# Eight experts' feed-forward part on one core: all experts for all tokens, against tokens scattered to their two experts in 46 tiles of 128 slots

## The chip, the core and the metric

One core of one Trainium2 chip. The time is that of one whole execution on the device in microseconds (us); several executions are timed and their median is given. Engines: TensorE (PE; its weight loads are PEld), VectorE (DVE), ScalarE (ACT), GpSimd (POOL), and SyncE (SP), which issues DMAs. A small q behind an engine's name means its sequencer.

## What is computed

x has 4 x 512 tokens of 256 features, all fp32. The first half is attention with 16 heads (4 key/value heads) of 128: softmax attention with rotary positions and a gated linear recurrence, averaged, projected back, added to x and normalised. The second half, which the change rewrites, is:

```python
routing_weights = softmax(x @ gate_w.T)              # 8 experts
top_w, top_idx = top_k(routing_weights, 2)
comb[t, top_idx] = top_w                             # zero for the six others
g = einsum('td,edf->etf', x, w_gate)                 # F = 176 features an expert
u = einsum('td,edf->etf', x, w_up)
y = einsum('etf,efd->etd', silu(g) * u, w_down)
out = layernorm(x + einsum('te,etd->td', comb, y))
```

## The kernel before

The five engines have a program each, written in order, and meet only at semaphores. Most fp32 products are done as three fp32r products: of the high parts, and of each high part with the other's low part (`_hi`, `_lo`). So each operand needs a copy that rounds to the high part and a subtraction that makes the low part.

**Attention.** 16 groups g (4 batches by 4 key/value heads), 4 steps c of 128 tokens each; unit u = 4g + c. Group 0 and group 15 are written out, groups 1 to 14 are a loop on each engine. In a step TensorE does, in this order: `score` (L405, L414), `gla_matrix` (L423), `gate_sums` (L375), `project` of step c+2 (L362), `output` of step c-1 (L434), `turn_weights` (transposes of the softmax weights, L443), `turn` (transposes of q, k for the next step, L386 to L395), `gather` (L452, L461) and the state's update (L465). VectorE: row maxima (L838), scaling of the weights (`normalise`, L872), `add_output` into `acc` (L903), and the low parts; its step ends with `k_out`, `q_low` and `log_gates`. GpSimd: `weigh_features` (L1227), `move_v`, `decay` (L1239), `rotate` (L1216, L1219), `x_split`. In groups 0 and 15 `decay` (L893) and `move_v` are VectorE's instead. In group 15 GpSimd splits the FFN's weights (L1273, L1280), loaded by SP, and VectorE and GpSimd normalise the first 512 tokens.

**FFN.** Four groups n of 512 tokens; the 8 x 176 features are taken as 11 blocks f of 128, which cut across experts. For each (n, f) TensorE computes `gate_up` (12 matmuls of 512 columns, L547), spreads the routing weights over the features (`spread_comb`, L555) and adds `down` of block f-2 (12 matmuls of 256 columns, L567) in PSUM bank PR. ScalarE: silu (L757) and the high part of h (L763). VectorE: two products (L1090, L1096) and the low part (L1102). Each group's normalisation and routing (transposes, logits, rank of each expert L1067 to L1072, weights) run between the blocks of the group before. The last group's sum, second normalisation and two output DMAs follow the last `down` (L1183 to L1202, L337 to L340).

## Time and profile before

| | us |
|---|---|
| runs | 1077.69, 1073.81, 1077.68; median 1077.68 |
| profiled execution | 1077.24 |
| its span, first to last instruction | 1075.5 |
| busy: PE, PEld, DVE, ACT, POOL | 1007.1, 802.7, 759.4, 627.2, 633.1 |
| mean granted TensorE clock | 0.988 |

The span is the profile's; the time of an execution is 1.7 us more. Matmuls overlap, so what a matmul costs is read from the distance of two starts and not from its duration. An idle time in square brackets stands ahead of the instruction, with what ended it. The three attention groups before group 15 go from 655.5 to 807.5 us, counted by `add_output`; the FFN's first matmul starts at 858.87.

### The profile page before, as it was taken

How to read it: one execution, taken by the hardware profiler on the slowest of the kernel's cores; microseconds unless marked ns; L12 is line 12 of the kernel's file. 1: busy time of each engine (PE TensorE's matmuls, PEld its weight loads, DVE VectorE, ACT ScalarE, POOL GpSimd, SP SyncE). 2: the span in 40 equal slices, each digit the busy share in tenths (PEclk: the TensorE clock that was granted, in tenths of full speed). 3: DMA queues.
4: the chain of work that ended last, by engine and by line, in shares of the span. 5: the costliest groups of instructions: out<-in, count | busy, mean ns of one | idle time of the engine just before them, and what ended most of it. 6: DMA issues, size and time to landing. Idle time of an engine off the chain costs nothing.

```text
span 1075.5 us, 20731 instructions
## 1 busy us (share of the span) xinstructions
PE 1007.1 (94%) x5860; PEld 802.7 (75%) x5860; DVE 759.4 (71%) x1741; ACT 627.2 (58%) x1944; POOL 633.1 (59%) x656
## 2 busy tenths in 40 slices
PE   4699999999999999999999999999997999999996
PEld 3567777677777777777777776777775688888886
DVE  4888767677676767676767776776769765767655
ACT  4456666666766667666666666667665334333321
POOL 5678676767666767676676767676659560202000
PEclk8899999999999999999999999999999999999999
DMA  7110000000000000000000000000002110000001
GB/s 234 50 50 25 11 10 10 10 10 15 10 10 10 10 10 10 10 11 13 10 10 10 10 10 10 10 15 10 25 0 74 58 45 1 1 21 1 20 1 40
DMA packets 26095, 24.07 MB, mean 22 GB/s; under 512 B 1744, under 2 KB 22608, under 8 KB 25936
## 3 DMA queue, kind: packets, MB, share of 16 engines
q1 hardware_dynamic: 26064, 23.67, 7.3%
q8 instruction: 17, 0.28, 0.1%
q14 instruction: 14, 0.11, 0.0%
HBM read 21.57 MB, written 2.10 MB: 22 GB/s over the span
## 4 chain that ended last, share of the span: by engine, by line
PE 79%; DVE 12%; ACT 5%; issue 3%; DMA 0%; DVEq 0%; POOLq 0%; POOL 0%; SPq 0%
PE OA L461 11%; PE S L547 11%; PE PR L362 10%; PE S L414 8%; PE S L443 6%; PE MS L434 6%; PE PR L567 6%; PE OA L452 4%; PE OA L423 4%; DVE pr L872 3%; ACT eqk L671 3%; PE PR L390 3%; PE PR L386 2%; PE MS L375 2%; DVE qd L893 2%
## 5 line engine op out<-in xcount | busy, mean ns | idle before, releaser
L644 ACT ACTIVATE pr<-S,nm 128x128 f32<-128x128 f32 (+3 forms) x256 | 131.5, 524 | 94.4 <-DVE nm L838 92.6
L1239 POOL TENSOR_TENSOR qd<-eqk,eg 128x512 f32<-128x512 f32 x56 | 68.0, 1215 | 177.9 <-issue 151.7
L461 PE MATMUL OA<-wT,V 128*128 128x512 f32 x320 | 149.3, 596 | 1.4 <-DVE wT L920 1.4
L671 ACT ACTIVATE eqk<-qkv,nmx 128x128 f32<-128x128 f32 x320 | 124.3, 395 | 8.4 <-DVE nmx L912 8.3
L1216 POOL TENSOR_TENSOR rp<-qkv,cos 128x640 f32<-128x640 f32 x64 | 100.8, 1575 | 30.9 <-ACT qkv L661 22.4
L838 DVE TENSOR_REDUCE nm<-S 128x2 f32<-128x256 f32 (+3 forms) x128 | 101.9, 818 | 21.8 <-PE S L414 20.0
L872 DVE TENSOR_SCALAR pr<-pr,rl 128x128 f32<-128x128 f32 (+3 forms) x256 | 110.2, 473 | 4.5
L461 PEld LDWEIGHTS OA<-wT,V 128*128 128x128 f32 x320 | 59.5, 190 | 72.1 <-issue 68.9
L1219 POOL TENSOR_TENSOR rp<-rp,rt 128x640 f32<-128x640 f32 x64 | 99.0, 1547 | 5.0
L1216 POOL TENSOR_TENSOR rt<-qkv,sin 128x640 f32<-128x640 f32 x64 | 98.9, 1545 | 0.0
L443 PE MATMUL S<-cm,pr 128*128 128x128 f32 x640 | 81.9, 275 | 15.7 <-DVE pr L872 15.7
L692 ACT COPY wT<-S 128x512 f32<-128x512 f32 x96 | 51.7, 592 | 67.5 <-PE S L443 67.5
L443 PEld LDWEIGHTS S<-cm,pr 128*128 128x128 f32 x640 | 71.4, 142 | 19.1 <-DVE pr L872 19.1
L362 PE MATMUL PR<-w_hi,ring_hi 128*128 (+2 forms) x256 | 78.0, 386 | 7.8 <-DVE w_lo L1131 6.9
L1227 POOL TENSOR_TENSOR eqk<-eqk,rse 128x640 f32<-128x640 f32 x56 | 72.2, 1290 | 20.8 <-PE OA L461 10.6
L763 ACT CAST wo_hi<-eqk 128x512 fp32r<-128x512 f32 x44 | 27.3, 620 | 90.2 <-DVE eqk L1096 90.2
L1310 POOL TENSOR_TENSOR rstd<-ve,neghalf 128x4 f32<-128x4 f32 x7 | 7.2, 1024 | 123.1 <-DVE ve L1031 123.1
L434 PE MATMUL MS<-wo_hi,oT_hi 128*128 (+1 forms) x256 | 74.1, 289 | 5.4 <-DVE gc L880 5.4
L362 PE MATMUL PR<-w_hi,ring_lo 128*128 (+2 forms) x256 | 73.7, 370 | 0.0
L434 PE MATMUL MS<-wo_hi,oT_lo 128*128 (+1 forms) x256 | 72.3, 282 | 0.0
L434 PE MATMUL MS<-wo_lo,oT_hi 128*128 (+1 forms) x256 | 72.2, 282 | 0.0
L547 PE MATMUL S<-ring_hi,w_hi 128*128 128x512 f32 x176 | 70.3, 399 | 0.0
(180 smaller groups left out, 2972.9 us busy)
## 6 DMA issues: line engine op xcount, KB each, us to landing
xraw<-in_x_cols SPq DMA_DIRECT2D x64, 128.0 KB, 2.2
stage<-in_wffn SPq DMA_DIRECT2D x11, 384.0 KB, 3.1
stage<-in_wqkv SPq DMA_DIRECT2D x6, 384.0 KB, 3.3
acc<-in_x_rows SPq DMA_DIRECT2D x1, 2048.0 KB, 12.6
out<-pr SPq DMA_DIRECT2D x3, 512.0 KB, 2.9
wT<-in_wo_in SPq DMA_DIRECT2D x1, 1024.0 KB, 6.5
pr<-in_wqkv SPq DMA_DIRECT2D x2, 384.0 KB, 4.0
stage<-in_wo_in SPq DMA_DIRECT2D x2, 384.0 KB, 3.2
```

The source lines that it names most:

```text
L362: last = pe.matmul(PR[:, a:b], x[:, cc, k, :], wq_cols(w, kv, k, a, b), start=(i == 0), stop=(i == len(steps) - 1))
L414: last = pe.matmul(S[:, h, 0:n], q[:, h * 128:(h + 1) * 128], k[:, 0:n], start=False, stop=(i == len(steps) - 1), skip_group_check=True)
L434: last = pe.matmul(MS[:, 0:HID], o[:, h * 128:(h + 1) * 128], r, start=(i == 0), stop=(i == len(steps) - 1))
L443: last = pe.transpose(S[:, j, h * 128:(h + 1) * 128], pr[:, h, j * 128:(j + 1) * 128], ident)
L461: last = pe.matmul(OA[:, :], V[:, j, :], wT[:, j, :], start=(c == 0 and j == 0), stop=(j == c))
L547: last = pe.matmul(S[:, 2 * q + q0 % 2, :], w[:, f, k, q, :], x[:, n % 2, k, :], start=(i == 0), stop=(i == len(steps) - 1))
L644: nc.scalar.activation(pr[:, h, 0:n], S[:, h, 0:n], ACT.Exp, bias=nm[:, h:h + 1], scale=1.0, accum_out=ls[:, h:h + 1]).then_inc(s_exp, 1)
L671: last = nc.scalar.activation(eqk[:, par, h * 128:(h + 1) * 128], qkv[:, c % C, h * 128:(h + 1) * 128], ACT.Exp, bias=nmx[:, h:h + 1], sca ...
L838: nc.vector.tensor_reduce(nm[:, 2 * pair:2 * pair + 2], S[:, 2 * pair:2 * pair + 2, 0:n], AX_X, ALU.max, negate=True).then_inc(s_nm, 1)
L872: nc.vector.tensor_scalar(pr[:, h, 0:n], pr[:, h, 0:n], rl[:, h:h + 1], None, ALU.mult).then_inc(s_pn, 1)
L1216: nc.gpsimd.tensor_tensor(to.rearrange("p (h w d) -> p h w d", w=2, d=64), src, tab, ALU.mult).then_inc(s_rt, 1)
L1219: nc.gpsimd.tensor_tensor(rp[:, c % 2, :], rp[:, c % 2, :], rt[:, :], ALU.add).then_inc(s_rp, 1)
```

## The change

- **Routing first.** The loop now covers groups 1 to 11 (`PEEL` = 12); groups 12 to 15 are written out, with step number k = 0 to 15. The first normalisation, transposes, logits, ranks and sums of token tiles 0 to 11 (three batches) are put into these steps at numbered places (`STATS_AT`, `TURN_AT`, ...). Tokens are counted for each expert by a scan and two matmuls (`prefix`), and each expert's slots are rounded up to tiles of 128.
- **Slots.** Set 0 (12 token tiles) has 31 slot tiles, set 1 (4 token tiles) 15: the most that rounding can need. GpSimd scatters each normalised token tile by two indirect DMAs (`send`) to its slots in device memory (`slot_x`), which SP has cleared. 24 of them stand in steps k = 12, 13, 14.
- **FFN by slot tile.** SP loads tile q, TensorE turns it (`turn_x`), reads the tile's expert number from `te` into a register (`value_load`) and uses it to address the weights: `gate_up` 6 matmuls of 352 columns, `turn_h` 2 transposes, `down` 6 matmuls of 256 columns into OA. No work is done on other experts' features. The result goes through ScalarE (`y_out`) and SP to `slot_y`.
- **Gather.** GpSimd fetches the two rows of each token (`fetch`, two indirect DMAs a tile); VectorE adds them with their weights (`combine`), from slot tile 36 on for token tiles 0 to 11; the last four follow all slot tiles. ScalarE does the second normalisation in place.
- **Weights.** The 16 matrices of the experts are split by ScalarE (`wide_high`) and VectorE (`wide_low`) in steps 4 to 14 and after the first tile, no longer by GpSimd. In group 15 GpSimd does `decay` and `move_v` itself.

```diff
+TPB = N // P128
+PEEL = NG - 4
+SETS = ((0, 3 * TPB), (3 * TPB, TILES))
+SLOT_TILES = [((b - a) * P128 * 2 + E * (P128 - 1)) // P128 for a, b in SETS]
+NT_A, NT_B = SLOT_TILES
+NT = NT_A + NT_B
...
+        wide = [("g", 0), ("g", 1), ("d", 0), ("d", 1), ("g", 2), ("g", 3), ("d", 2), ("d", 3),
+                ("g", 4), ("g", 5), ("d", 4), ("d", 5), ("g", 6), ("g", 7), ("d", 6), ("d", 7)]
+        WIDE_AT = (4, 5, 6, 7, 8, 9, 10, 10, 11, 12, 13, 13, 14, 14, 16, 16)
+        n_gu = max(i for i, (kind, _) in enumerate(wide) if kind == "g") + 1
+        TURN_AT = {2: 0, 3: 1, 4: 2, 5: 3, 6: 4, 7: 5}
+        LOGITS_AT = {k + 1: p for k, p in TURN_AT.items()}
+        STATS_AT = {0: 0, 2: 1, 4: 2}
+        NORM_AT = {k + 1: n for k, n in STATS_AT.items()}
+        RANK_AT = {5: 0, 7: 1, 9: 2}
+        EXP_AT = {k + 1: n for k, n in RANK_AT.items()}
+        PREFIX_AT, SLOTS_AT, WEIGH_AT = 10, 11, 13
+        SEND_AT = {12: (0, 4), 13: (4, 8), 14: (8, 12)}
...
+            def clear_slots(s, a, b):
+                sp.dma_start(slot_x[s].rearrange("(n p) d -> p n d", p=P128)[:, a:b, :],
+                             zero[:, :].rearrange("p (o n) -> p o n", o=1).to_broadcast([P128, b - a, HID])).then_inc(s_zf, 16)
...
+            def load_slots(q):
+                if q == 0:
+                    sp.wait_ge(s_sent[0], 16 * 2 * MOST[0])
+                    sp.wait_ge(s_v, NU - 2)
+                    sp.wait_ge(s_rp, NU - 2)
+                    sp.wait_ge(s_gl, NU - 2)
+                if q == NT_A:
+                    sp.wait_ge(s_sent[1], 16 * 2 * MOST[1])
+                later(sp, s_tx, q - 3)
+                sp.dma_start(xg[:, q % 4, :], slot_rows(slot_x, q)).then_inc(s_xg[q % 4], 16)
+            def store_slots(q):
+                sp.wait_ge(s_yo, q + 1)
+                sp.dma_start(slot_rows(slot_y, q), yo[:, q % 3, :]).then_inc(s_y[q % 3], 16)
...
+            def logits(xT, tiles, to):
+                for i in range(tiles):
+                    for k in range(KT2):
+                        last = pe.matmul(to[:, i * E:(i + 1) * E], xT[:, (KT2 * i + k) * 128:(KT2 * i + k + 1) * 128],
+                                         gate_w[:, k * E:(k + 1) * E], start=(k == 0), stop=(k == KT2 - 1))
+                last.then_inc(s_lgm, 1)
...
+                if k in LOGITS_AT:
+                    pe.wait_ge(s_gate, 16)
+                    pe.wait_ge(s_xe, LOGITS_AT[k] + 1)
+                    logits(x1T, 2, MS[:, 256:384])
+                if k == PREFIX_AT:
+                    prefix(0, MS[:, 256:384])
...
+                if k in TURN_AT:
+                    pe.wait_ge(s_am, C * g + c + 1)
+                    turn_tokens(TURN_AT[k], OA)
...
+            def turn_x(q):
+                pe.wait_ge(s_xg[q % 4], 16 * (q // 4 + 1))
+                if q < 2:
+                    pe.wait_ge(s_qdT, NU)
+                    pe.wait_ge(s_rql, 3 * NG)
+                later(pe, s_txl, q - 1)
+                for k in range(KT2):
+                    last = pe.transpose(xside(q)[:, k * 128:(k + 1) * 128], xg[:, q % 4, k * 128:(k + 1) * 128], ident)
+                last.then_inc(s_tx, 1)
+            def gate_up(q):
+                if q == 0:
+                    pe.wait_ge(s_flo, n_gu)
+                    pe.wait_ge(s_te, 1)
+                if q == NT_A:
+                    pe.wait_ge(s_te, 2)
+                expert[q] = pe.value_load(te[0:1, q:q + 1], min_val=0, max_val=E - 1)
+                pe.wait_ge(s_txh, q + 1)
+                pe.wait_ge(s_txl, q + 1)
+                later(pe, s_h, q - 1)
+                steps = [(k, x, w) for k in range(KT2) for x, w in ((xT_hi, gu_hi), (xT_hi, gu_lo), (xT_lo, gu_hi))]
+                for i, (k, x, w) in enumerate(steps):
+                    last = pe.matmul(S[:, q % 2, 0:2 * F], x[:, q % 2, k * 128:(k + 1) * 128],
+                                     expert_cols(w, expert[q], k * 2 * F, (k + 1) * 2 * F),
+                                     start=(i == 0), stop=(i == len(steps) - 1))
+                last.then_inc(s_gu, 1)
+            def turn_h(q):
+                pe.wait_ge(s_h, q + 1)
+                later(pe, s_hl, q - 1)
+                pe.transpose(S[:, 2 + q % 2, 0:128], hbuf[:, q % 2, 0:128], ident)
+                pe.transpose(S[0:TAIL, 2 + q % 2, 128:256], hbuf[:, q % 2, 128:F], ident).then_inc(s_th, 1)
+            def down(q):
+                if q == 0:
+                    pe.wait_ge(s_flo, len(wide))
+                    pe.wait_ge(s_oTl, NU)
+                pe.wait_ge(s_hh, q + 1)
+                pe.wait_ge(s_hl, q + 1)
+                later(pe, s_yo, q)
+                steps = [(k, h, w) for k in range(2) for h, w in ((hT_hi, dn_hi), (hT_hi, dn_lo), (hT_lo, dn_hi))]
+                for i, (k, h, w) in enumerate(steps):
+                    rows = TAIL if k else P128
+                    last = pe.matmul(OA[:, 0:HID], h[0:rows, q % 2, k * 128:(k + 1) * 128],
+                                     expert_cols(w[0:rows], expert[q], k * HID, (k + 1) * HID),
+                                     start=(i == 0), stop=(i == len(steps) - 1))
+                last.then_inc(s_dn, 1)
...
+            for q in range(1, NT + 2):
+                if q + 1 < NT:
+                    turn_x(q + 1)
+                if q < NT:
+                    gate_up(q)
+                if q >= 2:
+                    down(q - 2)
+                if q - 1 < NT:
+                    turn_h(q - 1)
...
+            def x_hi(q):
+                act.wait_ge(s_tx, q + 1)
+                later(act, s_gu, q - 1)
+                nc.scalar.copy(xT_hi[:, q % 2, :], PR[:, (q % 2) * 512:(q % 2) * 512 + 256]).then_inc(s_txh, 1)
+            def silu(q):
+                act.wait_ge(s_gu, q + 1)
+                later(act, s_h, q - 1)
+                nc.scalar.activation(sg[:, q % 2, :], S[:, q % 2, 0:F], ACT.Silu).then_inc(s_sg, 1)
+            def h_hi(q):
+                act.wait_ge(s_th, q + 1)
+                later(act, s_dn, q - 1)
+                nc.scalar.copy(hT_hi[:, q % 2, :], S[:, 2 + q % 2, 0:256]).then_inc(s_hh, 1)
+            def y_out(q):
+                act.wait_ge(s_dn, q + 1)
+                later(act, s_y[q % 3], 16 * (q // 3))
+                nc.scalar.copy(yo[:, q % 3, :], OA[:, 0:HID]).then_inc(s_yo, 1)
...
+            def wide_low(i):
+                dve.wait_ge(s_fhi, i + 1)
+                _, hi, lo, _ = wide_job(i)
+                nc.vector.tensor_tensor(lo, wide_stage(i), hi.bitcast(F32), ALU.subtract).then_inc(s_flo, 1)
...
+                if k in STATS_AT:
+                    moments(STATS_AT[k])
+                if k in RANK_AT:
+                    route_rank(RANK_AT[k], 2 * RANK_AT[k] + 2)
+                    if RANK_AT[k] == 2:
+                        count_before(0)
+                if k == PREFIX_AT:
+                    slot_bases(0)
+                if k == SLOTS_AT:
+                    slots(0)
+                if k == WEIGH_AT:
+                    route_weigh(0)
+                for i in range(len(wide)):
+                    if WIDE_AT[i] == k:
+                        wide_low(i)
...
+            def x_lo(q):
+                dve.wait_ge(s_txh, q + 1)
+                nc.vector.tensor_tensor(xT_lo[:, q % 2, :], PR[:, (q % 2) * 512:(q % 2) * 512 + 256],
+                                        xT_hi[:, q % 2, :].bitcast(F32), ALU.subtract).then_inc(s_txl, 1)
+            def multiply(q):
+                dve.wait_ge(s_sg, q + 1)
+                later(dve, s_th, q - 1)
+                nc.vector.tensor_tensor(hbuf[:, q % 2, :], sg[:, q % 2, :], S[:, q % 2, F:2 * F], ALU.mult).then_inc(s_h, 1)
+            def h_lo(q):
+                dve.wait_ge(s_hh, q + 1)
+                nc.vector.tensor_tensor(hT_lo[:, q % 2, :], S[:, 2 + q % 2, 0:256],
+                                        hT_hi[:, q % 2, :].bitcast(F32), ALU.subtract).then_inc(s_hl, 1)
+            def combine(t):
+                a = acc[:, t, :]
+                dve.wait_ge(s_yg[t % 4], 32 * (t // 4 + 1))
+                nc.vector.scalar_tensor_tensor(out=a, in0=yg[:, t % 4, 0, :], scalar=wts[:, 0, t:t + 1], in1=a, op0=ALU.mult,
+                                               op1=ALU.add).then_inc(s_c0, 1)
+                dve.wait_ge(s_c0, t + 1)
+                nc.vector.scalar_tensor_tensor(out=a, in0=yg[:, t % 4, 1, :], scalar=wts[:, 1, t:t + 1], in1=a, op0=ALU.mult,
+                                               op1=ALU.add).then_inc(s_cb, 1)
+                dve.wait_ge(s_cb, t + 1)
+                norm_stats(2, t)
...
+                if not first:
                     pool.wait_ge(s_cp, C * g + c + 1)
                     pool.wait_ge(s_o, C * g + c)
-                    weigh_features(g, c + 1)
+                    if not (last and c == 3):
+                        weigh_features(g, c + 1)
                     move_v(g, c)
-                    decay(g, c + 1)
+                    if not (last and c == 3):
+                        decay(g, c + 1)
...
+                if k in NORM_AT:
+                    norm1(NORM_AT[k])
+                if k in SEND_AT:
+                    for t in range(*SEND_AT[k]):
+                        send(t)
...
+            def send(t):
+                s = 0 if t < SETS[0][1] else 1
+                if t == SETS[s][0]:
+                    pool.wait_ge(s_sl, s + 1)
+                    pool.wait_ge(s_zf, 64)
+                    pool.wait_ge(s_x1a, SETS[s][1])
+                for r in range(2):
+                    nc.gpsimd.indirect_dma_start(slot_x[s], bass.IndirectOffsetOnAxis(ap=sloti[:, r, t:t + 1], axis=0),
+                                                 acc[:, t, :], None).then_inc(s_sent[s], 16)
+            def fetch(t):
+                if t == 0 or t == SETS[1][0]:
+                    for i in range(3):
+                        pool.wait_ge(s_y[i], stored(NT_A if t == 0 else NT, i))
+                later(pool, s_cb, t - 3)
+                for r in range(2):
+                    nc.gpsimd.indirect_dma_start(yg[:, t % 4, r, :], None, slot_y[0 if t < SETS[0][1] else 1],
+                                                 bass.IndirectOffsetOnAxis(ap=sloti[:, r, t:t + 1], axis=0)).then_inc(s_yg[t % 4], 16)
```

On TensorE, in the middle of the FFN, one block f of before was this; the rows are instructions in order, and L555 is the spreading of the weights.

```order
L555 MATMUL MS<-w_hi,w_lo 128x512
L547 MATMUL S<-ring_hi,w_hi 128x512
L547 MATMUL S<-ring_hi,w_lo 128x512
L547 MATMUL S<-ring_lo,w_hi 128x512
...
L567 MATMUL PR<-wo_hi 128x256
L567 MATMUL PR<-wo_lo,wo_hi 128x256
L567 MATMUL PR<-wo_hi,wo_lo 128x256
```

The three L547 rows stand four times and the three L567 rows four times. A slot tile of after, on the same engine (L686 `down`, L673 `turn_h`, L650 `turn_x`, L665 `gate_up`; ISA and REGISTER_ALU are the sequencer's):

```order
L686 ISA
L686 MATMUL OA<-wo_hi,rq_hi 128x256
L686 REGISTER_ALU
L686 MATMUL OA<-wo_lo,rq_hi 128x256
...
L673 MATMUL S<-cm,rp 128x128
L674 MATMUL S<-cm,rp 48x128
L650 MATMUL PR<-cm,qkv 128x128 x2
L659 TENSOR_LOAD te
L659 ISA x2
L665 ISA
L665 MATMUL S<-w_hi,ring_hi 128x352
```

Twelve matmuls and four transposes stand where 25 matmuls stood, and between `turn_x` and `gate_up` the expert number is loaded. On VectorE the end of a peeled step, k = 9 of after, between its last old instruction (`log_gates`, L1088) and the next step:

```order
L1088 SCALAR_TENSOR_TENSOR gl<-qkv,lnp 128x128
L1131 TENSOR_REDUCE small<-lg 128x4
L1133 TENSOR_TENSOR lx<-lg,small 128x32
L1140 TENSOR_TENSOR rk<-lg 128x256
L1142 TENSOR_TENSOR rk<-lg 128x256
L1143 TENSOR_TENSOR rk<-rk,tri 128x256
L1145 TENSOR_TENSOR rk<-rk 128x256
L1147 TENSOR_REDUCE rank<-rk 128x32
L1150 TENSOR_SCALAR picked<-rank 128x4x8
L1155 SCALAR_TENSOR_TENSOR run<-cm,picked 128x96
L1156 TENSOR_TENSOR before<-run,picked 128x96
L1218 TENSOR_TENSOR w_lo<-stage,w_hi 128x704
```

In before nothing stands there. On GpSimd, steps k = 12 to 14:

```order
L1416 TENSOR_TENSOR rp<-rp,rt 128x640
L1512 DMA slot_x<-acc,sloti 3968x256 x8
L1424 TENSOR_TENSOR eqk<-eqk,rse 128x640
L1445 COPY V<-qkv 128x128
L1436 TENSOR_TENSOR qd<-eqk,eg 128x512
L1440 TENSOR_TENSOR qd<-eqk,eg 128x128
L1413 TENSOR_TENSOR rp<-qkv,cos 128x640
```

Eight indirect DMAs stand ahead of the next step's `weigh_features` (L1424) and `decay` (L1436).

## Rows read from the trace of the kernel before

**Rows 1.** The page's chain that ended last, by engine.

```profile
PE 79%; DVE 12%; ACT 5%; issue 3%; DMA 0%; DVEq 0%; POOLq 0%; POOL 0%; SPq 0%
```

**Rows 2.** Busy us (instructions) of PE, PEld, DVE, ACT, POOL; clock; DMA share, GB/s.

```profile
822.00:860.00 38.00, 31.68 (x158) 23.33 (x159) 32.05 (x75) 16.26 (x46) 26.86 (x30) 0.96 0.21 61
...
910.00:962.00 52.00, 52.00 (x301) 45.62 (x300) 34.65 (x77) 18.42 (x30) 7.36 (x6) 1.00 0.03 11
```

**Rows 3.** Groups by shape from 800 us on: count, busy us, mean ns, idle before.

```profile
L1102 DVE TENSOR_TENSOR wo_lo<-eqk,wo_hi 128x512 fp32r<-128x512 f32 x44 | 31.9, 724 | 30.2 <-ACT wo_hi L763 30.2
...
L763 ACT CAST wo_hi<-eqk 128x512 fp32r<-128x512 f32 x44 | 27.3, 620 | 90.2 <-DVE eqk L1096 90.2
...
L1022 DVE BATCH_NORM_STATS2 st<-acc 128x6 f32<-128x256 f32 x16 | 5.6, 409 | 0.0
...
L1067 DVE TENSOR_TENSOR rk<-lg 128x256 f32<-128x256 f32 x4 | 1.7, 419 | 0.0
```

**Rows 4.** TensorE in order of time: start us, us, line, operation, count.

```profile
452.13 0.60 PE L443 MATMUL S<-cm,pr 128*128 128x128 f32 x4
452.56 0.60 PE L386 MATMUL PR<-cm,rp 128*128 128x128 f32 x4
...
858.87 0.79 PE L547 MATMUL S<-ring_hi,w_hi 128*128 128x512 f32 x1
...
951.78 0.39 PE L547 MATMUL S<-ring_hi,w_hi 128*128 128x512 f32 x1
952.00 0.39 PE L547 MATMUL S<-ring_hi,w_lo 128*128 128x512 f32 x1
...
953.66 0.28 PE L567 MATMUL PR<-wo_lo,wo_hi 128*128 128x256 f32 x1
953.78 0.28 PE L567 MATMUL PR<-wo_hi,wo_lo 128*128 128x256 f32 x1
...
1067.30 0.28 PE L567 MATMUL PR<-wo_hi,wo_lo 128*128 128x256 f32 x1
```

**Rows 5.** VectorE in order of time, `add_output` of units 31, 34, 47, 59, 62.

```profile
452.53 0.42 DVE L903 SCALAR_TENSOR_TENSOR acc<-MS,acc 128x256 f32 x1 [1.86 <-PE MS L434]
...
490.09 0.42 DVE L903 SCALAR_TENSOR_TENSOR acc<-MS,acc 128x256 f32 x1 [0.95 <-PE MS L434]
...
655.50 0.43 DVE L903 SCALAR_TENSOR_TENSOR acc<-MS,acc 128x256 f32 x1 [1.87 <-PE MS L434]
...
807.50 0.42 DVE L903 SCALAR_TENSOR_TENSOR acc<-MS,acc 128x256 f32<-128x256 f32 x1 [0.37 <-PE MS L434]
...
852.39 0.41 DVE L903 SCALAR_TENSOR_TENSOR acc<-MS,acc 128x256 f32<-128x256 f32 x1
```

**Rows 6.** In order of time: last scalings of a step, and TensorE's turning after them.

```profile
437.50 0.88 DVE L872 TENSOR_SCALAR pr<-pr,rl 128x512 f32<-128x512 f32 x2
...
439.00 1.15 PE L443 MATMUL S<-cm,pr 128*128 128x128 f32 x9
...
463.58 1.09 PE L443 MATMUL S<-cm,pr 128*128 128x128 f32 x8 [0.80 <-DVE pr L872]
```

**Rows 7.** Line L362, sequencer's own steps: ns min/median/max, first and last start us.

```profile
L362 PEldq FUSED_REGOPS  x112: 46/51/108, 92.1 to 776.1; - x112
L362 PEldq ALU_OP  x112: 32/32/32, 92.4 to 776.3; - x112
```

**Rows 8.** A GpSimd group of the page; a DMA's landing us; its issue on SP.

```profile
L1216 POOL TENSOR_TENSOR rp<-qkv,cos 128x640 f32<-128x640 f32 x64 | 100.8, 1575 | 30.9 <-ACT qkv L661 22.4
...
xraw<-in_x_cols SPq DMA_DIRECT2D x64, 128.0 KB, 2.2
...
834.14 0.33 SPq L306 DMA_DIRECT2D stage<-in_csel  x1
```

**Rows 9.** VectorE and GpSimd beside each other, in order of time.

```profile
461.01 0.62 DVE L872 TENSOR_SCALAR pr<-pr,rl 128x256 f32<-128x256 f32 x2
...
461.74 1.79 DVE L872 TENSOR_SCALAR pr<-pr,rl 128x256 f32<-128x256 f32 x2
...
461.67 1.29 POOL L1239 TENSOR_TENSOR qd<-eqk,eg 128x512 f32<-128x512 f32 x1 [1.60 <-issue]
```

889 lines of the change are left out of this document (444 added, 445 removed).

## The prediction

> **What bounds the kernel now.** I read first the chain of waits [rows 1]: TensorE holds 79% of the span, VectorE 12%. Then the busy time by stage [rows 2]: in the middle of the feed-forward part (FFN) TensorE is busy 52.00 of 52.00 us, so there only its own work counts. Then the shapes of FFN and routing instructions [rows 3], TensorE in order of time [rows 4], and VectorE's `add_output` (L903), the clock of the attention steps [rows 5]. Three dividing points follow: attention groups 0 to 11 are over at 655.5 us, the last step begins its output near 852.4, the FFN's first matmul starts at 858.9, its last at 1067.3 (over at 1067.6), and the span ends at 1075.5. So the FFN lasts 208.7 us and the tail 7.9. The profiled execution took 1077.24 us, 1.7 above its span; the median of the runs is 1077.68, so a sum made against this execution needs no correction.
>
> In attention three groups last 152.0 us, 50.7 each (655.5 to 807.5) [rows 5]. TensorE has nearly no idle time there, but VectorE is close behind: its last softmax scaling of a step (L872) ends at 438.38 and TensorE's turning of those weights starts at 439.00, 0.6 us of slack, and at step c=1 TensorE already waits 0.80 us for it [rows 6].
>
> **FFN, TensorE's own work.** Starts of matmuls are 0.22 us apart at 512 columns and 0.12 at 256; four transposes take 0.43, so 0.11 each [rows 4]. By the line through the first two, 352 columns cost 0.16. Before, a step f has 12 matmuls of 512, 12 of 256 and the spreading of the weights: about 4.4 us, 44 times. After, a tile of 128 slots has 6 of 352 (0.98), 6 of 256 (0.72) and 4 transposes (0.44): 2.14 us, 46 times, 98 us. If TensorE alone counted, the FFN would fall from 208.7 to about 98.
>
> **FFN, what takes its place.** A tile runs through ScalarE four times and VectorE three, and the output bank OA is single. The loop from one `down` to the next: 6 matmuls 0.72, their drain (a 256-column matmul lasts 0.28 where the next starts after 0.12 [rows 4]) and the hand-over 0.28, `y_out` 0.3 to the start of `h_hi`, `h_hi` 0.4 (a 512-column cast is 0.62 [rows 3], so 0.4 for 256 is an estimate), hand-over 0.06, `h_lo` 0.42 (as L903 [rows 5]), hand-over 0.1 (the hand-overs are estimates): 2.28 us. A second loop is TensorE's sequencer, which stands still at a wait of several semaphores and then issues `down`, `turn_h`, `turn_x`, the load of the expert number into a register, and `gate_up`: 16 matmuls at about 0.055 and some 11 register steps of 0.03 to 0.1 [rows 7], 1.7 us, plus the register load from on-chip memory, L. No such load stands in the trace. Lower bound: a register step, 0.1 us. Upper bound: a 128 KB DMA from issue to landing, 2.2 us [rows 8]. I take L = 1.0, between a local step and a round trip. Period: the longer of 2.28 and 1.7 + L, so 2.7 us; 2.28 at the lower bound, 3.9 at the upper. 46 x 2.7 = 124 us.
>
> The Trainium skill ("DMA: Bandwidth & Descriptors", section "Latency and other measured facts") gives a `tensor_load` a floor of about 600 ns. With that figure the period would be about 2.3 and my sum 18 us lower (an estimate); no row here shows such a load.
>
> On top of 124 come: waiting for the last two expert matrices' low parts before the first `down`, 3; in the first 13 tiles the routing of the last 4 token tiles, about 11 us on VectorE, 4 on TensorE and two table loads on ScalarE, of which I take 10 as exposed; in the last 12 tiles the weighted sum of two gathered rows (two 0.42 and one 0.41 statistics, links between, about 1.4 to 1.9 us on VectorE), which brings the loop over VectorE to about 3.1 us, 5 us more in all. FFN: 142 us, against 208.7: **-67**.
>
> **The four peeled groups.** Groups 0 to 11 keep their code and their 655.5 us; the new constants at the start I cost at nothing (under 1 us if DMA cover is missing). Steps k = 0 to 15 take new work. TensorE: six times 4 transposes (0.43) and 4 small fp32 matmuls (two weight loads of 0.11 each at least, so 0.9, an estimate), prefix sums 1: 9 us. VectorE: three sets of moments (4 x 0.41 and aggregates, 2.1 each), three rankings (five of 0.42 and three of 0.2, 3.0 each), 14 low parts of weights (0.72 for 512 columns, about 0.9 for 704), slot bases 2.1, slots 2.0, weights 1.9: about 36 us [rows 3]. VectorE has room in a step, but these stand at the step's end, ahead of the next step's maxima, where the slack is 0.6 us or less, and some 3.3 only ahead of c=0. Step by step (own work less slack, less what TensorE's new work covers) I get about 22 us exposed for k = 0 to 11 and 6 for 12 to 14. Bounds: 11 if all but TensorE's own work hides, 45 if nothing does. I take **+28**, nearest to the step-by-step row.
>
> GpSimd loses the splitting of weights and in the last group takes the decay products back from VectorE. There from 807.5 to 852.4 go 44.9 us; the same three steps in the steady state (452.53 to 490.09) take 37.6 [rows 5]. **-8** with the little that follows.
>
> **Sending the tokens.** GpSimd issues 24 indirect stores, 8 after each of steps 12, 13, 14, and each batch stands ahead of the next step's `weigh_features` and `decay`, for which TensorE's `turn` waits. GpSimd's chain from step 12's start to `turn_x(0)`: three steps' own work (its rotations are 1.58 us each [rows 8]) and waits 20, landing and first slot load 4.5, so 24.4 + 24T, T being one indirect DMA on GpSimd. TensorE needs about 49 for the same stretch: 6 up to `add_output`, the 37.6 above, 6 exposed. T has no row either: a plain DMA's issue on SP took 0.33 us, and the landing 2.2 [rows 8]. I take T = 1.2, near the middle: 53 against 49, **+5**; nothing at T = 1.0 or less, +28 at 2.2. The clearing of slots (6 MB) and their loads by SP run beside steps of 12 us and four tiles ahead of use: nothing; without that cover a few us.
>
> **The tail.** Last `down`, copy 0.5, store landed 2.4, eight gathers 8T = 9.6, landing 2.2, last sum 1.3, moments, root, shift, normalising 2.3, output 2.7: 21 us against 7.9, **+13**.
>
> **Sum:** 1077.2 - 67 + 28 - 8 + 5 + 13 = 1048, and I say **1049 us**, 2.6% faster.
>
> **Rivals.**
> 1. The register load decides (ends slower). If L is 1.8 us or more the period is 3.5 to 3.9 and the FFN 37 to 55 us longer: 1086 to 1104. It turns slower from a period of 3.3 (L = 1.6). For it: 2.2 us for a DMA; against it: the sequencer's other steps cost 0.03 to 0.1 [rows 7].
> 2. Indirect DMAs are dear on GpSimd: T = 2.2 gives +23 at the sends, +8 in the tail, and gathers slower (4.4 us a tile) than the last tiles, +10: about 1090. For it: when the two engines meet, both are held up: two equal scalings, 0.62 us for the pair, took 1.79 when GpSimd ran beside [rows 9]. The Trainium skill ("SBUF — State Buffer", section "Who interferes with whom") says that GpSimd cannot write descriptors while VectorE runs copies or scalings in a 2-port mode; by that rule VectorE's scalings would lengthen T. The trace agrees that such pairs wait for each other; for descriptors no run shows it yet.
> 3. Everything hides: L under 0.6 and a third of the 28 gone: 1049 - 18 - 9 = 1022.
> 4. The granted clock falls in the FFN to the lower level, as it did for part of the last group (a mean of 0.96 from 822 to 860 us, where TensorE was busy 31.68 of 38 us, against 1.00 in the FFN [rows 2]). At 1.2 GHz a tile is 4.3 us on TensorE: +74, 1123. Against: gaps here are under 1 us each.
>
> **How the numbers follow.** My forecast (1030 to 1072) 0.52, rival 1 0.16, rival 2 0.14, rival 3 0.10, rival 4 0.04, and 0.04 for a mixture near no change. A difference under 0.5% is about what a measurement of this kernel can't tell from none. Faster: forecast and rival 3, 0.61; same 0.07; slower 0.32. The range reaches down to rival 3 and up into rivals 1 and 2: 1020 to 1098; the forecast's own is 1030 to 1072.
>
> **What would show it.** Tiles' first `gate_up` matmuls 2.7 us apart (2.3: L is small; 3.5: rival 1, with TensorE idle by "issue"). The FFN's start near 884 us against 858.9. `add_output` in steps 48 to 59 spread over about 174 us instead of 152. GpSimd's 24 sends ending before TensorE asks for tile 0, or a wait of `turn_x(0)` for it. From the last `down` to the end 21 us. The prediction is wrong if the peeled steps cost over 45 us, or if the period is not set by the sequencer or the loop over OA.

## The result and the profile after

The changed kernel takes 1081.67 us (median of 17 runs, 1078.98 to 1085.5) against 1077.69 for the kernel before: the ratio is 1.0043 with a 95% interval from 1.0025 to 1.0061, so it is 0.4% slower. I had forecast 1049. The profiled execution has a span of 1081.3 us.

The busy time by stage of the kernel after, to be laid beside [rows 2]: groups 1 to 11, peeled steps 0 to 11, the rest of attention, the first 15 slot tiles, the steady tiles, the last ones, the tail. Columns: the stretch and its length; busy us (instructions) of PE, PEld, DVE, ACT, POOL; granted clock; DMA share, GB/s.

```profile
99.10:657.40 558.30, 540.89 (x3212) 421.56 (x3211) 396.77 (x946) 378.62 (x1254) 388.69 (x397) 1.00 0.05 15
657.40:851.20 193.80, 168.64 (x956) 132.17 (x955) 134.46 (x344) 112.27 (x360) 125.65 (x124) 0.94 0.14 43
851.20:908.00 56.80, 46.22 (x215) 35.41 (x214) 33.37 (x79) 26.77 (x77) 38.58 (x39) 0.82 0.29 97
908.00:966.10 58.10, 50.91 (x270) 43.66 (x268) 26.65 (x91) 25.27 (x65) 10.84 (x10) 0.82 0.21 64
966.10:1026.00 59.90, 59.85 (x370) 50.04 (x369) 27.15 (x74) 30.57 (x92) 9.89 (x11) 1.00 0.41 124
1026.00:1051.00 25.00, 21.49 (x126) 16.91 (x124) 20.41 (x65) 12.67 (x38) 19.71 (x21) 1.00 0.55 157
1051.00:1081.30 30.30, 4.50 (x14) 3.08 (x14) 11.03 (x36) 6.61 (x15) 10.91 (x13) 0.51 0.39 124
```

What to see: the feed-forward part (FFN) and tail are 173.3 us instead of 216.6, so it did shrink. But steps 0 to 11 take 193.8 us instead of 152, at a clock of 0.94, and in the two stretches behind them TensorE has both idle time and a clock of 0.82, where [rows 2] showed 0.96 and 1.00. Of the 41.8 us that the steps grew, 20 are TensorE's idle time (25.2 us against 4.9 in the same twelve steps of before) and 21.5 are busy time. My sum had about 9 of these as its new work; the other 12 are what a clock of 0.94 costs over 193.8 us (an estimate: 6% of it).

The chain that ended last, for [rows 1], by engine:

```profile
PE 66%; DVE 15%; ACT 8%; issue 6%; POOL 3%; DMA 1%; DVEq 0%; ACTq 0%; SPq 0%; POOLq 0%
```

TensorE's waits from 657 to 908 us (engine, tile and line, who was waited for: us in total, times, longest):

```profile
PE OA L524 <- DVE oT_lo L960: 16.2, 6, 3.8
PE MS L476 <- DVE gl L1088: 11.3, 4, 3.4
PE PR L650 <- DMA qkv<-slot_x: 2.6, 1, 2.6
...
PE S L544 <- DVE pr L1002: 0.7, 1, 0.7
```

I had looked for the loss at the softmax scaling (`pr`), with 0.6 us of slack [rows 6]. It is not there. TensorE waits for `oT_lo` (which frees bank OA for the next step) and for `gl` (the gates). Both stand close behind the new work: `oT_lo` is the first thing that VectorE does in the steps c=2 and c=3 (in c=0 it comes behind one row maximum), and in a step c=1 the gates come behind two row maxima. Here is VectorE in order of time at the longest of these waits, the turn from step k=5 to k=6 (start us, us, engine, line, operation; in brackets idle time before and its releaser):

```profile
737.40 0.19 DVE L1085 RECIPROCAL rse<-se 128x5 f32<-128x5 f32 x1 [1.09 <-ACT eqk L780]
738.28 0.29 DVE L1088 SCALAR_TENSOR_TENSOR gl<-qkv,lnp 128x128 f32<-128x128 f32 x1 [0.70 <-ACT lnp L793]
...
739.86 1.43 DVE L1143 TENSOR_TENSOR rk<-rk,tri 128x256 f32<-128x256 f32 x1
...
742.47 0.89 DVE L1218 TENSOR_TENSOR w_lo<-stage,w_hi 128x704 fp32r<-128x704 f32 x1
743.27 0.68 DVE L960 TENSOR_TENSOR oT_lo<-OA,oT_hi 128x512 fp32r<-128x512 f32 x1
...
744.01 0.94 PE L524 MATMUL OA<-qdT,kdT 128*128 128x512 f32 x1 [3.84 <-DVE oT_lo L960]
```

VectorE first stands idle for 1.09 and 0.70 us ahead of `rse` and `gl`, then ranks and splits weights from 738.5 to 743.3, and only then makes `oT_lo`, for which TensorE has been waiting 3.84 us. The slack is in the step, and the new work stands behind it. Two smaller things add to it. The ranking product L1143 lasts 1.43 us where its neighbours take 0.42, beside a GpSimd product from 739.75 to 741.01; such holds come up again below. And in two of the twelve steps VectorE waits for ScalarE's high part of a weight matrix, 4.3 us in all, 3.2 of them shortly ahead of a wait of 3.4 us for `gl` at 795: a hand-over that my sum did not have.

### The profile page after: what moved, and what is told of

Same layout as the page of the kernel before. It is cut to its first block, busy times and chain, and to the rows that moved or that the text cites. A ratio compares the mean times of both kernels' runs of the same rounds, so it can differ in the third digit from the quotient of the medians.

```text
span 1081.3 us, 20494 instructions
## 1 busy us (share of the span) xinstructions
PE 962.3 (89%) x5516; PEld 756.3 (70%) x5516; DVE 725.0 (67%) x1772; ACT 643.9 (60%) x2060; POOL 670.9 (62%) x689
## 4 chain that ended last, share of the span: by engine, by line
PE 66%; DVE 15%; ACT 8%; issue 6%; POOL 3%; DMA 1%; DVEq 0%; ACTq 0%; SPq 0%; POOLq 0%
PE OA L562 9%; PE PR L463 9%; PE MS L535 7%; PE S L515 7%; PE S L544 6%; PE OA L686 5%; ACT eqk L780 5%; PE S L665 4%; PE OA L524 3%; PE OA L555 3%; DVE pr L1002 3%; PE PR L491 2%; PE PR L487 2%; PE MS L476 2%; DVE gl L1088 2%
## 5 line engine op out<-in xcount | busy, mean ns | idle before, releaser
L1436 POOL TENSOR_TENSOR qd<-eqk,eg 128x512 f32<-128x512 f32 x59 | 71.9, 1219 | 187.8 <-issue 167.1
L1002 DVE TENSOR_SCALAR pr<-pr,rl 128x128 f32<-128x128 f32 (+3 forms) x256 | 107.4, 462 | 4.5
L1424 POOL TENSOR_TENSOR eqk<-eqk,rse 128x640 f32<-128x640 f32 x59 | 75.8, 1285 | 35.6 <-DVE rse L1085 20.8
L544 PE MATMUL S<-cm,pr 128*128 128x128 f32 x640 | 84.7, 282 | 11.4 <-DVE pr L1002 11.4
L544 PEld LDWEIGHTS S<-cm,pr 128*128 128x128 f32 x640 | 74.4, 145 | 14.1 <-DVE pr L1002 14.0
L524 PE MATMUL OA<-qdT,kdT 128*128 128x512 f32 x128 | 68.6, 618 | 16.3 <-DVE oT_lo L960 16.2
L535 PE MATMUL MS<-wo_hi,oT_hi 128*128 (+1 forms) x256 | 77.1, 301 | 5.0 <-DVE gc L1010 4.5
L535 PE MATMUL MS<-wo_hi,oT_lo 128*128 (+1 forms) x256 | 73.9, 289 | 0.0
L535 PE MATMUL MS<-wo_lo,oT_hi 128*128 (+1 forms) x256 | 73.8, 288 | 0.0
L463 PE MATMUL PR<-w_lo,ring_hi 128*128 (+2 forms) x256 | 70.1, 356 | 0.0
L515 PE MATMUL S<-KT_hi,rq_hi 128*128 128x256 f32 (+2 forms) x192 | 68.9, 359 | 0.0
```

The lines of the kernel that those rows point to most:

```text
L463: last = pe.matmul(PR[:, a:b], x[:, cc, k, :], wq_cols(w, kv, k, a, b), start=(i == 0), stop=(i == len(steps) - 1))
L515: last = pe.matmul(S[:, h, 0:n], q[:, h * 128:(h + 1) * 128], k[:, 0:n], start=False, stop=(i == len(steps) - 1), skip_group_check=True)
L524: pe.matmul(OA[:, :], kdT[:, :], qdT[:, c % 2, :], start=True, stop=True).then_inc(s_at, 1)
L535: last = pe.matmul(MS[:, 0:HID], o[:, h * 128:(h + 1) * 128], r, start=(i == 0), stop=(i == len(steps) - 1))
L544: last = pe.transpose(S[:, j, h * 128:(h + 1) * 128], pr[:, h, j * 128:(j + 1) * 128], ident)
L1002: nc.vector.tensor_scalar(pr[:, h, 0:n], pr[:, h, 0:n], rl[:, h:h + 1], None, ALU.mult).then_inc(s_pn, 1)
```

## Experiments on the peeled steps

**Place within the step.** One version moves the extras, in the same steps: on VectorE `extras(k)` (moments, ranking, slot arithmetic, low parts) from the end of `step` to just ahead of `log_gates` (for c = 0 ahead of `add_output`), on ScalarE `router_exp` and `wide_high` ahead of `weights_out` (the excerpt shows VectorE's part).

```diff
+                if c == 0:
+                    extras(k)
                 ...
                 add_output(...)
                 ...
+                if c:
+                    extras(k)
                 if n2 and c:
                     log_gates(g, c + 2)
-                if k in STATS_AT:
-                    moments(STATS_AT[k])
-                ...
```

> The same work in the same steps, at another place within the step. VectorE's extras stand ahead of the gates' logarithm step, where VectorE waits about 1.6 us a step for ScalarE, instead of behind it (in steps with c = 0 ahead of add_output, where it waits for TensorE); ScalarE's weight copies and router exponentials stand ahead of its copies of the turned weights, where it waits for TensorE, instead of at the step's end. Theory A (place within the step decides): TensorE's waits for oT_lo and gl in steps 48 to 62 fall from about 27 us to under 12, the clock falls less, the feed-forward part starts 15 to 30 us earlier, 1052 to 1067 us. Theory B (VectorE has simply too much to do in these steps, and the place changes only who waits): within 5 us of 1081.7.

Measured: 1063.88 us, ratio to the kernel before 0.9867 [0.9831, 0.9904]; the FFN starts at 890.3 us instead of 908.0. Its waits of TensorE from 659 to 890:

```profile
PE PR L491 <- POOL qd L1446: 9.0, 3, 6.1
PE MS L495 <- DVE acc L1033: 4.4, 4, 2.8
PE OA L524 <- DVE oT_lo L960: 4.2, 2, 2.5
...
PE MS L476 <- DVE gl L1088: 2.1, 3, 0.9
```

The waits for `oT_lo` and `gl` fall from 27.5 to 6.3 us: theory A. No work was taken away, and 18 us are gone. The version moves both engines' extras, so what each engine's move is worth alone is not shown. A new wait came instead, for GpSimd's decay products: 6.11 us at 851.6 where a batch of eight sends stood ahead of them. So the sends, which had cost 2.6 us (one wait of `turn_x`) while other things were late, became the next bound as soon as VectorE was not.

**Less work in the step.** The copies and differences of expert weights cut to 8 columns, everything else as in the changed kernel:

```diff
-                nc.scalar.copy(wide_job(i)[1], wide_stage(i)).then_inc(s_fhi, 1)
+                nc.scalar.copy(wide_job(i)[1][:, 0:8], wide_stage(i)[:, 0:8]).then_inc(s_fhi, 1)
```

> ScalarE's high copy and VectorE's low difference of each of the 16 expert matrices take 8 columns instead of 704 or 512; semaphores, DMAs and everything else stay. Left out: the splitting of the expert weights, so what the feed-forward part multiplies by is not the weights. Theory A (the extras at the end of a step hold up the next step, whoever they are): ScalarE loses 0.76 us and VectorE 0.88 us in each of ten steps, so TensorE's waits of 2 to 4 us for the output low part and for the gates shrink by about 1.5 us each where a matrix stood; the feed-forward part starts 10 to 20 us earlier than 908, the kernel takes 1062 to 1072 us against 1081.7. Theory B (the ranking and the slot arithmetic alone are what is late): under 6 us earlier, 1076 to 1082.

Measured: 1068.81 us, 0.9926 [0.9897, 0.9955]; steps 0 to 11 take 185.7 us instead of 193.8 and the FFN starts at 900.0. The time is in the range of theory A, the start 2 us short of it. So all the weight splitting is worth 13 us where it stands. In the profiled run 8 us of the gain are ahead of the FFN, where moving it and the rest within the step brings 17.7. Another 7 us are in the first 15 slot tiles (50.7 us instead of 58.1), which hold the last two splits but also vary from version to version, as comes below.

**How much of it is the clock.** The changed kernel with filler on TensorE: 16 to 48 meaningless bf16 products (0.06 us each) ahead of the long waits, 252 in all, some 15 us of work added.

```diff
+        FILL_AT = {5: 36, 6: 48, 9: 36, 10: 48, 11: 16, 13: 36, 14: 32}
...
+                if k in FILL_AT:
+                    ...
+                    fill(FILL_AT[k], PR[:, 0:128], 128)
                 if c:
                     gla_matrix(g, c)
```

> TensorE does 16 to 48 meaningless bf16 matmuls of 128 columns (into a bank that is free there) ahead of the place where it waited 2 to 4 us, in seven steps between 48 and 61: it adds about 1 to 3 us of work in front of each long wait and nothing else. Theory A (a large part of the loss is the granted clock, which is 0.94 from 657 to 851 us and 0.82 up to the feed-forward part, some 22 us of TensorE work at full rate): the clock stays nearer 1.00 there and the feed-forward part starts 5 to 15 us earlier, though TensorE does more. Theory B (the waits alone cost the time and the lower clock falls into them): the start is unchanged or up to 10 us later, since part of the added work lies on the path.

Measured: 1072.79 us, 0.9946 [0.993, 0.9963], 9 us less than the changed kernel; the FFN starts at 901.6. The busy time up to there:

```profile
658.40:844.80 186.40, 171.07 (x1141) 135.28 (x1140) 134.85 (x344) 111.85 (x360) 126.09 (x124) 0.99 0.15 45
844.80:901.60 56.80, 46.36 (x283) 35.48 (x282) 33.50 (x79) 26.71 (x77) 38.91 (x39) 0.91 0.29 97
```

The clock is 0.99 and 0.91 where it was 0.94 and 0.82, and steps 0 to 11 are 7.4 us shorter with more work on TensorE: theory A. The last group keeps its 56.8 us, so there the better clock only paid for the added work. In the changed kernel TensorE ran at the lower of its two levels (1.2 GHz, a granted share of 0.50) after a wait of 3.3 us at 724; this is the stretch behind it, and the one before the wait. Products of L535 start 0.21 us apart in it (729.76, 729.97, 730.18), and the same products of before 0.12 us (L434, 450.72 and 450.83):

```profile
724.00:734.00 10.00, 9.74 (x43) 9.55 (x44) 5.47 (x14) 3.64 (x12) 9.05 (x10) 0.50 0.08 21
704.00:723.00 19.00, 16.96 (x105) 12.88 (x103) 11.29 (x35) 10.83 (x38) 15.28 (x16) 1.00 0.00 1
```

So this wait cost more than its own length.

**Spreading.** On top of the early place: group 11 peeled too (20 steps), the tables of steps thinned out so that no step gets more than one or two pieces, and the 24 sends two to four at a time.

```diff
-PEEL = NG - 4
+PEEL = NG - 5
-        WIDE_AT = (4, 5, 6, 7, 8, 9, 10, 10, 11, 12, 13, 13, 14, 14, 16, 16)
+        WIDE_AT = (3, 4, 5, 8, 8, 9, 9, 10, 10, 11, 13, 13, 14, 14, 16, 16)
-        RANK_AT = {5: 0, 7: 1, 9: 2}
+        RANK_AT = {2: 0, 3: 1, 6: 2}
-        PREFIX_AT, SLOTS_AT, WEIGH_AT = 10, 11, 13
+        PREFIX_AT, SLOTS_AT, WEIGH_AT = 7, 7, 11
-        SEND_AT = {12: (0, 4), 13: (4, 8), 14: (8, 12)}
+        SEND_AT = {8: (0, 1), 9: (1, 3), 10: (3, 5), 11: (5, 6), 12: (6, 8), 13: (8, 10), 14: (10, 12)}
```

> The early place within the step, and the same extras spread over 20 steps instead of 16 (group 11 is written out too): the moments of tokens finished earlier start four steps sooner, no step with c = 0 or 1 gets more than one or two pieces, slots are ready after step k=7, and the 24 sends go out two to four at a time in seven steps instead of eight at a time in three. Theory A (in the version with the early place what is left is the block of eight sends, 1.26 us each, ahead of GpSimd's decay products, for which TensorE waited 6.1 and 2.8 us): those waits vanish and the feed-forward part starts 10 to 18 us earlier than the 890.3 of that version, 1046 to 1054 us. Theory B (TensorE's own added work and GpSimd's total of work set these steps): the waits on GpSimd spread with the sends and the start stays at 884 to 890, 1058 to 1064.

> The same spreading over 20 steps, but every extra at the end of its step, as in the changed kernel. Theory A (place and amount both count): between the two, the feed-forward part starts 8 to 20 us later than with the early place and the same spreading, about 1062 to 1072 us. Theory B (only the amount in a step and the batches of sends matter): within 4 us of the version with the early place. Theory C (only the place matters): no better than the changed kernel but for the sends, 1074 or more.

Measured: spread and early 1061.33 us, 0.9849 [0.9805, 0.9894]; spread and late, as in the changed kernel, 1078.13, 1.0006 [0.9979, 1.0034]. The place is worth 17 us here and 18 with the old tables, so for the late version theory C holds; the spreading brings about 3 us (2.6 and 3.5), hardly more than the runs vary. The FFN starts at 889.5 us: hardly earlier than the 890.3 of the early version, a miss for my theory A, since a third wait had appeared. The spread version, VectorE and GpSimd in order of time:

```profile
803.52 6.46 DVE L1002 TENSOR_SCALAR pr<-pr,rl 128x384 f32<-128x384 f32 x2
803.67 1.27 POOL L1430 TENSOR_TENSOR eqk<-eqk,rse 128x640 f32<-128x640 f32 x1
...
805.29 1.08 POOL L1442 TENSOR_TENSOR qd<-eqk,eg 128x512 f32<-128x512 f32 x1
806.34 0.44 POOL L1446 TENSOR_TENSOR qd<-eqk,eg 128x128 f32<-128x128 f32 x1
806.75 1.52 POOL L1419 TENSOR_TENSOR rp<-qkv,cos 128x640 f32<-128x640 f32 x1
808.24 1.52 POOL L1419 TENSOR_TENSOR rt<-qkv,sin 128x640 f32<-128x640 f32 x1
809.84 1.55 POOL L1422 TENSOR_TENSOR rp<-rp,rt 128x640 f32<-128x640 f32 x1
809.90 0.41 DVE L1033 SCALAR_TENSOR_TENSOR acc<-MS,acc 128x256 f32<-128x256 f32 x1
...
810.04 1.69 PE L544 MATMUL S<-cm,pr 128*128 128x128 f32 x8 [4.95 <-DVE pr L1002]
```

Two scalings that take 0.41 us each alone last 6.46 us together, 1.65 and 4.89, and the second ends 0.2 us behind the start of the first gap in GpSimd's row (0.08 us, ahead of L1422 at 809.84). The first got through beside GpSimd's copy L1451 (804.88 to 805.32) although no gap stood there. TensorE waits 4.95 us. It happens once more at 849.9 (4.95 us, TensorE waits 5.79). Four sends ahead had made GpSimd late, so that its products and rotations, otherwise parted by waits, stood in one row.

**What holds the scaling.** First the same scaling in another form, a product of two tensors, in steps k = 7 to 14:

```diff
-                    nc.vector.tensor_scalar(pr[:, h, 0:n], pr[:, h, 0:n], rl[:, h:h + 1], None, ALU.mult).then_inc(s_pn, 1)
+                    nc.vector.tensor_tensor(pr[:, h, 0:n], pr[:, h, 0:n], rl[:, h:h + 1].to_broadcast([P128, n]),
+                                            ALU.mult).then_inc(s_pn, 1)
```

> The spread version, with VectorE's scaling of the softmax rows in steps k = 7 to 14 written as a product of two tensors instead of a tensor times a scalar. In the spread version two such scalings (0.42 us alone) took 4.89 and 4.95 us while GpSimd ran sends, decay products and rotations without a gap, and TensorE waited 4.95 and 5.79 us for them. Theory A (this form of the scaling, and not the other, is kept out for as long as GpSimd runs back to back): each is 0.5 to 0.7 us in the other form, the two long waits vanish, and the feed-forward part starts 6 to 11 us earlier, less about 0.2 us for each of the 32 slower scalings that is on the path; 1052 to 1058 us. Theory B (the time is a wait for something else that ends with GpSimd's run): the waits of 5 us stay, whatever the form, 1060 or more.

Measured: 1064.43 us, 0.9885 [0.9853, 0.9918]. Theory A fell: the two last 5.09 and 5.08 us, TensorE waits 5.21 and 6.12. The form does not matter: theory B. Next, with the FFN order of the next section, gaps on GpSimd: in steps k = 7 and later it waits for itself between the two decay products, ahead of the rotation and within it.

```diff
+                if gap:
+                    pool.wait_ge(s_qd, 2 * u + 1)
                 nc.gpsimd.tensor_tensor(qd[:, par, 512:640], eqk[:, par, 512:640], eg[:, par, 130:258],
```

> The reordered version with waits of GpSimd on itself between its two decay products, ahead of its first rotation product and between the two rotation products, in steps k = 7 and later: these four instructions followed each other without a gap, 805.3 to 809.8 us, and the scaling on VectorE that began at 805.1 ended at 809.9. Theory A (an operation of VectorE among on-chip rows that begins beside GpSimd is held until GpSimd pauses): each of the two scalings ends at the first gap, 1 to 2 us instead of 4.9, TensorE's two waits of 4.94 and 5.80 fall to under 3, and the feed-forward part starts 4 to 8 us earlier than 889.1. Theory B (they share access in turn, and the length follows from the total of GpSimd's work beside it, or the cause is another engine): 4.9 us stay.

The same place in that version:

```profile
803.33 3.08 DVE L1002 TENSOR_SCALAR pr<-pr,rl 128x384 f32<-128x384 f32 x2
...
805.11 1.08 POOL L1446 TENSOR_TENSOR qd<-eqk,eg 128x512 f32<-128x512 f32 x1
806.27 0.46 POOL L1452 TENSOR_TENSOR qd<-eqk,eg 128x128 f32<-128x128 f32 x1
...
806.47 1.53 PE L544 MATMUL S<-cm,pr 128*128 128x128 f32 x12 [1.56 <-DVE pr L1002]
```

GpSimd's gap is 0.08 us (806.19 to 806.27), and the held scaling ends there instead of 3.6 us later. The longest single scaling from then on is 2.3 us, TensorE's waits for it are 4.9 us in all instead of 12.7, and the FFN starts at 884.6 instead of 889.1 in the same version without gaps. That is theory A, with a part of the gain going elsewhere: the waits for `gc` on VectorE are 6.3 us, where the spread version had 3.0. Whether any pause lets the other engine in, or only a row of products with two inputs holds it, is not shown; the copy above speaks for the second. The kernel as a whole took 1063.61 us, 0.9882 [0.9855, 0.9908], for a reason that comes below.

The Trainium skill ("SBUF — State Buffer", section "Who interferes with whom") says that the two engines share a pair of ports, that whoever issues first holds it for the whole instruction and the other blocks, and that a VectorE instruction with two on-chip inputs contends as well; by that the second form had to be held too, and was. What the trace adds is that the hold outlasted the instruction: 4.9 us over four instructions of GpSimd in a row, up to its first gap.

## Experiments on the feed-forward part

My sum had 142 us for the FFN (first matmul to the end of the last `down`); it took 150.9, of which the steady tiles are 2.60 us each (I said 2.7). The period was nearly right and the reason was not. One turn of the loop in the kernel after:

```profile
989.89 0.42 DVE L1303 TENSOR_TENSOR rq_lo<-S,rq_hi 128x256 fp32r<-128x256 f32 x1 [1.01 <-ACT rq_hi L877]
...
990.52 0.38 PE L686 MATMUL OA<-wo_hi,rq_hi 128*128 x1
...
991.61 0.33 PE L673 MATMUL S<-cm,rp 128*128 128x128 f32 x1
...
992.08 0.37 ACT L877 CAST rq_hi<-S 128x256 fp32r<-128x256 f32 x1
...
992.49 0.42 DVE L1303 TENSOR_TENSOR rq_lo<-S,rq_hi 128x256 fp32r<-128x256 f32 x1 [1.09 <-ACT rq_hi L877]
```

From low part to low part it is 2.60 us: low part of h, `down` (six matmuls, 1.09), turning of the next h, its high part, its low part. Three versions took this apart.

> The expert of tile q is the constant q modulo 8 instead of a number loaded into a TensorE register; the load, its register operations and the address arithmetic fall away. Left out: which expert's weights a tile is multiplied by. Theory A (TensorE's sequencer sets the tile period, as my sum said: 1.7 us plus the load): the period of tiles 15 to 38 falls from 2.6 us to the 2.3 of the loop over the output bank, so 8 to 12 us less, about 1071. Theory B (the loop over the output bank and the hand-overs already sets 2.6): period unchanged, within 2 us of 1081.7. The first 14 tiles stay at about 4 us under both.

```diff
-                expert[q] = pe.value_load(te[0:1, q:q + 1], min_val=0, max_val=E - 1)
+                expert[q] = q % E
```

Measured on the changed kernel: 1074.43 us, 0.9974 [0.9957, 0.999], 7 us less; the period of the steady tiles falls from 2.60 to 2.47, 3 us in them, and the first 15 tiles take 50.8 us instead of 58.1. These tiles took 50.7 us in the version with less weight splitting, with its register loads, so that difference can't be put down to the loads. The register load (0.30 us in the trace, and 0.15 of register steps) shows with 0.13 us a steady tile: more than theory B, a third of what theory A wanted.

> The spread version, with the down product of odd slot tiles from 17 on in bank MS, free by then, instead of in OA, so that a down product no longer waits for the copy of the one before. Theory A (the loop over the single output bank sets the tile period of 2.6 us): the period of tiles 18 to 38 falls to 2.1 to 2.3, 6 to 11 us less than the spread version. Theory B (TensorE's sequencer, with the register load, sets it: with constant experts it was 2.47): 2.5 to 2.6 still, under 2 us less.

```diff
-                    last = pe.matmul(OA[:, 0:HID], h[0:rows,
+                    last = pe.matmul(y_bank(q), h[0:rows,
+        def y_bank(q):
+            return (MS if q > TWO and q % 2 else OA)[:, 0:HID]
```

Measured: 1060.96 us, 0.9831 [0.9764, 0.9898], the spread version's time; the median period of tiles 18 to 38 is 2.59 against 2.60. The single output bank sets nothing: theory A fell.

> The spread version, with another order in the feed-forward part: TensorE turns h of tile q-1 ahead of the down product of tile q-2 instead of behind it, and ScalarE and VectorE make its high and low part ahead of the output copy of tile q-2. Neither a second output bank (2.58 us a tile) nor constant expert numbers (2.47) moved the tile period of 2.60 much. Theory A (the loop is down, turning of h, output copy or high part, low part, next down: 0.98 + 0.5 + 0.4 + 0.4 + hand-overs = 2.57 in the trace): the order takes the down product out of it, and the period of tiles 15 to 38 falls to TensorE's own 2.1 to 2.3, 7 to 12 us less than the spread version. Theory B (TensorE's sequencer: the period is its instructions and the register load): 2.45 to 2.6 still, under 3 us less.

```diff
-                if q >= 2:
-                    down(q - 2)
                 if q - 1 < NT:
                     turn_h(q - 1)
+                if q >= 2:
+                    down(q - 2)
```

and on ScalarE and VectorE `h_hi(q - 1)` and `h_lo(q - 1)` behind `silu(q)` and `multiply(q)`, ahead of `y_out(q - 2)`. Measured on top of the spread version: 1044.21 us, 0.9691 [0.9652, 0.9729], 17 us less. One tile of it on TensorE (first matmuls of the turning of x, of `gate_up`, of the turning of h, of `down`, and of the next tile):

```profile
955.45 0.44 PE L650 MATMUL PR<-cm,qkv 128*128 128x128 f32 x2
955.65 0.40 PE L665 MATMUL S<-w_hi,ring_hi 128*128 x1
...
956.70 0.27 PE L673 MATMUL S<-cm,rp 128*128 128x128 f32 x1
...
956.83 0.36 PE L686 MATMUL OA<-wo_hi,rq_hi 128*128 x1
...
957.91 0.44 PE L650 MATMUL PR<-cm,qkv 128*128 128x128 f32 x2
```

The period is 2.46 (2.9 in every fifth or sixth tile), and nothing but work is in it: 0.20 + 1.05 + 0.13 + 1.08. That is what I had put at 2.14. The period is in theory B's range, but a version below without register loads runs at 2.45, so it is not the sequencer; and neither theory had the 17 us. Only 1.4 us of the gain are in the steady tiles; 13.2 are in the first 15, 43.5 us instead of 56.7 in the spread version, and 3.3 in the last. (The first 15 took 53.4 to 56.7 us in five versions with the spread extras and the old order, so 10 to 13.) With the loop open, the routing of the last four token tiles beside them no longer stops TensorE, and the clock there is 1.00, where the spread version had 0.50 from 900 to 910 us and 0.84 behind it.

Filler in these first tiles, in the old order, does it less well:

> The spread version, with 12 to 24 meaningless bf16 matmuls of 128 columns in the first 13 slot tiles of the feed-forward part, where TensorE waits in the first two tiles and its clock was 0.50 from 900 to 910 us and 0.84 to 0.92 up to 940. Theory A (the first 14 tiles take 4.0 us each, not 2.6, largely since one of them is worked at 1.2 GHz after the waits of the first two): the clock stays at 1.00, the first 14 periods fall from 56 us in sum to 44 to 50. Theory B (routing of the last four token tiles on VectorE and the filling of the pipeline set them): the sum stays within 3 us of 56 or grows by the added work.

```diff
+            fill(24, S[:, 3, 0:128])
             for q in range(1, NT + 2):
+                if q == 1:
+                    fill(24, S[:, 3, 0:128])
+                if q in (2, 3):
+                    pe.wait_ge(s_acc, NU)
+                    fill(12, MS[:, 384:512])
+                ...
```

Measured: 1060.44 us, 0.983 [0.9807, 0.9853], against 1061.33 without it; the first 14 periods are 52.6 us in sum instead of 53.3. The clock is 1.00 in all of it but ten us at 0.83, and the added work takes what that gives: a draw, theory B. A better clock alone is therefore not what the new order brings there.

**The same order elsewhere.** I then made the one edit on the changed kernel itself, took the register loads out of the reordered version, and put the useful edits together with the tail's.

> The changed kernel with one edit: in the feed-forward part TensorE turns h of tile q-1 ahead of the down product of tile q-2, and its high and low part are made ahead of the output copy of tile q-2. If the order alone sets the period: 2.46 us a tile from tile 15 on instead of 2.60, the first 14 periods 43 us in sum instead of 56, and 1063 to 1068 us against 1081.7, faster than the kernel before. If the order only paid off with the attention part's clock restored (rival): the first 14 stay above 50 and the gain is under 6 us.

> The reordered version with constant expert numbers (the register load, its register operations and the address arithmetic fall away). Left out: which expert's weights a tile is multiplied by. If TensorE's sequencer sets the 2.46 us that are left: the period falls towards TensorE's own 2.14 and the kernel by 8 to 14 us. If another loop sets it (ScalarE's four operations, about 1.9 us with their waits, or the slots' loads): under 0.1 us a tile, under 4 us.

> The reordered version with the gaps on GpSimd, and at the end the sums of tiles 9 to 11 behind the last tile's low part with the first fetch of the last group ahead of GpSimd's root of the third. Without the gaps' gain 1041 to 1043, with it 1034 to 1039. If the moved sums are late themselves, no better than the gaps alone.

All three missed: 1088.72 us, 1.0085 [1.0049, 1.0121]; 1055.65, 0.9799 [0.9773, 0.9825]; 1062.28, 0.9854 [0.9834, 0.9875]. Their tiles run at 2.45 or 2.46 us, and then one takes 7 to 9 us at tile 16 and again at tile 36, with slow tiles at 1.2 GHz behind. On the changed kernel the first 15 tiles are shorter here too (46.4 us instead of 58.1), but the 23 behind them take 76 us instead of 60. In the version with constant expert numbers the tiles between take 2.45, so 2.46 is TensorE's own work, not the sequencer's. To tell whether it is the program or the moment:

> The same program as the reordered version (e9), a second time. If the stall at tiles 16 and 37 belongs to the program: none here, 1041 to 1049 us again. If it is a matter of the chip or of the moment: stalls of 7 to 9 us at tiles 16 and 37 here too, 1055 to 1062.

> The version with gaps on GpSimd (e13, 1063.6 us, stalls at tiles 16 and 37), with the eight sends of the last four token tiles held until slot tile 20 is copied out. Theory A (the sends and the gathers disturb ScalarE or its transfers): the first stall moves to tiles 21 to 24, the second stays with the first gather. Theory B (the place in ScalarE's program decides, as for instructions that come late from memory, 21 tiles apart): it stays at tile 16. If there is no stall at all, the time is 1038 to 1044.

```diff
             norm1(3)
+            pool.wait_ge(s_yo, 21)
             for t in range(3 * TPB, TILES):
                 send(t)
```

Measured: the same program as the 1044.21 us one took 1064.81, 0.988 [0.9856, 0.9903], on another chip, with the kernel before at 1077 on both (the three above, and the one with gaps, ran on a third). With the sends held back it is 1061.86, 0.9847 [0.9796, 0.9899]; its first stall is at tiles 25 to 28 (5.4, 5.3, 4.4 and 4.2 us), a little later than I expected and where the sends now run (951.6 to 961.5 us), and the second stays at tile 36, where the gathers begin. So the stalls go with GpSimd's indirect DMAs and not with a place in the program: theory A. The same stretch of time in the two runs of one program, first the one without the stall, then the one with it:

```profile
929.50:946.00 16.50, 16.27 (x105) 14.13 (x106) 8.80 (x29) 8.70 (x27) 7.84 (x8) 1.00 0.55 168
```

```profile
929.50:946.00 16.50, 11.60 (x59) 9.24 (x59) 5.98 (x22) 4.70 (x15) 7.83 (x8) 0.82 0.41 127
```

and ScalarE in order of time in the second:

```profile
934.94 0.37 ACT L867 CAST ring_hi<-PR 128x256 fp32r<-128x256 f32 x1 [1.08 <-issue]
939.93 0.32 ACT L872 ACTIVATE qd<-S 128x176 f32<-128x176 f32 x1 [4.63 <-remote]
```

GpSimd's eight sends (7.84 us) are there in both. In the second ScalarE starts late by 1 to 4.6 us for something that the profile does not name ("issue", "remote"). What it is, and why one chip shows it and another does not, stays open. All six reordered versions on two chips had it, and both on the third chip had not. No experiment with the old order ran on the two chips with the stall, so it is not shown either whether the order has a part in it or the chip alone. On the chip without it the old order took 1060.44 and 1064.43 us (with filler, with the other scaling), the new one 1044.21. I count the reordering as worth up to 17 us where the stall is absent. Where it is there, 1064.81 us is no better than the spread version's 1061.33, and the changed kernel loses 7; both are comparisons across chips.

**The tail.** From the last `gate_up` (1047.4) to the end the changed kernel takes 34 us. The chain there (start us, us, what):

```profile
1050.72 0.60 ACT acc L887
1052.18 0.34 DVE rq_lo L1303
1052.71 1.95 PE OA L686 x6
...
1055.46 0.59 ACT acc L887
...
1056.96 1.95 PE OA L686 x6
...
1059.34 1.76 DMA slot_y<-eqk
...
1061.36 1.01 POOL pr L1522
```

The last two `down` stand behind normalising (L887) and sums of earlier tiles, then come eight gathers, 0.96 us and 0.30 of issue each.

> The spread version, and at the end the weighted sums of token tiles 9 to 11 on VectorE and the normalising of tiles 4 to 7 on ScalarE stand behind the last tile's low part and copy instead of between them. Theory A (in the changed kernel TensorE's last two down products waited 2.42 and 1.70 us for VectorE's low part behind these, at the lower clock, and the store, fetch and last sums follow from the last product): last product, fetch and end come 3 to 5 us earlier than in the spread version. Theory B (the sums moved are then late themselves, since the fetch of tile 12 needs buffers freed by them): within 1 us.

> The spread version with the three edits of this set together (order in the feed-forward part, scaling form, filler in its first tiles), and at the end the sums of tiles 9 to 11 behind the last tile's low part, with the first fetch of the last four token tiles ahead of GpSimd's root of the third group (alone that move had put the fetch 3.7 us behind the last store's landing). If the gains add up (9, 8, 7 and 3 us): 1030 to 1040 us. If one of them takes another's slack: 1042 to 1055.

Measured: moving the sums alone, on the spread version, 1065.03 us, 0.9893 [0.9855, 0.9931]. Theory B: the last `down` ended earlier, but the first gather then waited for GpSimd's root, which waits for the moved sums, 3.7 us. With that gather ahead of the root, and with filler, form of the scaling and order as well (on the chip without the stall), 1050.33 us, 0.9733 [0.971, 0.9757]: from the last `gate_up` to the end 29.7 us against 32.3 in the reordered version, so 2.6 us for the tail. The whole is 6 us slower than the reordered version, so the other two edits cost about 9: the FFN starts 3.8 us later (892.9) with the other form of the scaling, and the first 15 tiles take 49.9 us instead of 43.5 with filler. Their own runs on the spread version, 3 us slower and 1 faster, had not said so much.

## Why the prediction was wrong, point by point

- **Start:** 657.4 us instead of 655.5; I had costed the new constants at nothing, under 1 us without cover. +2.
- **Peeled steps 0 to 11:** this is the step that failed, in the term +28. I said +22 for these and gave 45 as the bound; they cost +42 (193.8 against 152.0 us). The sum of the work was nearly right (36 us on VectorE, 39 in the trace), the slack was taken from the wrong row. I read the 0.6 us at the softmax scaling [rows 6] and took all slack to be there; the trace of before shows some 2.6 us a step of VectorE waiting ahead of `rse`, `gl` and `add_output`, which work at the step's end cannot use, and TensorE asking for `oT_lo` and `gl` at once behind it. The early place gives 18 us back. And I priced a wait at its length: about 12 of the 42 us are the clock's by its mean of 0.94 (an estimate), and the filler, with 15 us of work added, still made these steps 7.4 us shorter and the kernel 9. I had weighed the clock only for the FFN, as rival 4 with 0.04.
- **Last group up to the FFN:** 56.8 us against 54.5 by my steps; the -8 for the decay products did not show, eaten by waits of 2 to 3.3 us of the same kind and a clock of 0.82.
- **Sends:** T is 1.26 us (I took 1.2) and `turn_x(0)` waited 2.6 us (I said 5). Right, as long as VectorE was later than GpSimd; with VectorE out of the way they cost 9.
- **FFN:** 150.9 us against 142. Register load L = 0.30 us and not 1.0. The steady tiles are 2.60 and not 2.7, which is luck: neither the sequencer's 1.7 + L (2.0 with the measured L; its 0.055 us a matmul came from no row) nor the loop over OA sets them, but the loop from low part to low part, with `down` at 1.09 us where I had 0.72. The first 15 tiles took 58.1 us instead of 53.5 (15 x 2.7 and 13 on top), at a clock of 0.82, and the last eight, to the end of the last `down`, 33 instead of 26.6 (8 x 2.7 and 5). My floor of 2.14 for TensorE's own work was 2.46: `down` takes 1.08 us and not 0.72, since its matmuls of 256 columns start 0.12 or 0.20 us apart, and I had priced all at 0.12 from a row of the old FFN [rows 4]. The rule with a floor of about 600 ns for a register load (the Trainium skill, "DMA: Bandwidth & Descriptors", "Latency and other measured facts") is not borne out here: 0.30 us.
- **Tail:** 22.4 us from the end of the last `down`, against 21. Right.
- **Sum:** 2 + 20 + 2 + 9 + 1 = 34 us too low, against 1081.3 - 1046.3 = 35 in spans.
- **Rivals:** 1 (register load) and 3 fell. 2 was wrong in its price (a send took 0.96 to 1.23 us) and right in its neighbour: not the descriptors but VectorE's plain arithmetic is what was held beside GpSimd, as the 4.9 us show. 4 was right in kind and for the most part in the wrong stage: the steady tiles ran at 1.00, the peeled steps at 0.94 and the first 15 tiles at 0.82.
- **Signs:** two things stood as what would prove me wrong. That the period is set by neither the sequencer nor the loop over OA came true. The peeled steps at over 45 us stand at the bound: steps 0 to 11 cost 42, and from the end of group 11 to the FFN it is 250.6 us against 203.4, 47 more, 2.6 of them the wait of `turn_x(0)`; they are over the bound if the -8 came about.

The spread version with the early place beats both kernels, 1061.33 us, 1.5% faster than the kernel before. The reordered one is 3.1% faster or 1.2%, as the stall will have it.

## What to carry over

Put added work of an in-order engine ahead of the wait in which it stands idle, not at the end of a loop body: ask for each piece which operation of the next step it delays and who waits for that one first. A wait of TensorE of several us can cost more than its length: behind one of 3.3 us the granted clock was 0.50 for 10 us, so price a wait with the work that follows at half rate. When two engines share access, a late engine that runs without pauses can hold one operation of the other over several of its own instructions (4.9 us over four here); a pause of 0.08 us ended it.

## What I had not expected of the hardware

- A VectorE operation of 0.41 us took 4.89 and 4.95 us (and 5.09 in another form) beside a row of GpSimd products without a gap, and ended at the first gap, though it was 0.08 us wide.
- TensorE with 252 added matmuls was 9 us faster.
- One program, on two chips where the kernel before takes the same 1077 us, took 1044 and 1065 us.
- An indirect DMA of 128 rows costs GpSimd 0.96 us and 0.30 of issue, whether it scatters or gathers; a register load by TensorE 0.30 us.
